# A state-space mixer on one core: log of dt in the decay's bias, output halves summed in SBUF, y's parts first at unit changes, B and C projected a step sooner

## The chip, the cores and the metric

One Trainium2 chip, one core of it. The metric is the device time of one execution in microseconds; less is better. The kernel computes a two-layer network in one launch: attention, a quantized linear layer, a state-space mixer (SSD) and a mixture of low-rank experts, each with a residual and a layer norm behind it. 1024 tokens (2 sequences of 512), 512 channels.

## What is computed

Only the mixer is touched by the change. The reference, cut to it:

```python
dt = softplus(dt + dt_bias); dA = dt * A                    # A = -exp(A_log); 128 heads of 64, 8 groups
cum = cumsum(dA)                                            # within a chunk
Ldec[i, j] = exp(cum[i] - cum[j]) where j <= i, else 0
scores = (C @ B^T) * Ldec * dt[j];  y_intra = scores @ x
dlast = exp(cum[last] - cum); states = (dt * dlast * B)^T x;  cdec = exp(cum[last])
y_inter = (C * exp(cum)) @ state before the chunk;  y = y_intra + y_inter + D * x
g = y * silu(gate)                                          # gate, x, B, C: projections; x, B, C convolved with 4 taps
g = g * rsqrt(mean over the group's 1024 channels of g*g + eps) * norm_w
out = g @ out_w.T
```

## The kernel before, in words

The mixer runs 8 groups. A group has two units (halves) of 8 heads, 512 channels, and a unit walks over 8 chunks of 128 tokens, `c` = 0 to 7, four of each sequence. So a group is 16 steps, `k` = 0 to 15, with `half, c = divmod(k, CHUNKS)`, and the mixer is 128 steps. Each engine has its own list of these steps, written out by hand, and semaphores between them. Nothing reorders it: an engine that waits holds up all that stands behind in its list.

**PE** in a step: the gate projection of a later tile (12 matmuls of 512 columns), the carried part `p_inter` (state times C), one projection of x for the next unit (12), in some steps also one of B or C for the next group (12; `Plan` says in which: `extra`), then `project_out` of the step before (12, from `yT` and `w_out` to `p_out`), the chunk's state (`p_state`), the transposes of x (`p_flip`), and the step's own intra-chunk product (16 small matmuls to `p_intra`). At c = 0 and c = 7 the order is different: at k = 0 and 8 the gate projection comes first, then at once `project_out`; at k = 7 and 15 `project_out` comes behind the intra product.

**DVE** in a step: `mean_square` of two steps back; in half 1 `out_halves` (adds the unit's first half from SBUF to `p_out`, L1926); `arguments` of the next step (L1898: the smaller of two cumulated decays for 8 heads, one instruction of 1024 elements); in half 0 copies of B and C*B; `y_low_part` of the step before (L1908, the low part of y, which `project_out` waits for); `out_sum` (L1934: `p_out` times the inverse rms of the row, added to `acc`; it frees `p_out`); the carried part (L2000, L2005), the decay of the state (L2007), the convolution taps of what was projected (L806, 3 for each event), a copy for the next weights (`w_x`, L814), the new state (L2045, L2047), and `make_y` (L1945, L1950).

**ACT**: half of the decay exponentials (L1763, 8 of 128 columns, bias minus the own decay), `high_y` (L1738), the other half, then the silu of the gate (L1772), `square_y` (L1744), the last tap (L784), the silu of the convolution (L794), `keep_half` (L1748) in half 0, and `empty_x` (L1731). Exponentials and silu need different tables, so ACT loads a table twice in a step.

**POOL**: x with the weights of the state (`to_state`, L2121), x times dt (`to_scores`, L2126), x times D (`skip_part`, L2099), the inverse rms (L2090), the decay matrix times C*B (`decayed`, L2135, which the intra product waits for), the sums of squares (L2105, L2107), and in steps c = 3 to 6 the low parts of the next weights (L825, L2080).

```python
m = act.activation(decay[:, k % 2, h], decay[:, k % 2, h], ACT.Exp, bias=neg[:, c, head:head + 1])
dve.tensor_tensor(decay[:, k % 2], cumB[:], over(logs[:, 0, c, mine], P), ALU.min).then_inc(arg_done, 1)
pool.tensor_tensor(xdt[:], xtok[:], over(dtg[:, c, mine], HEAD_P), ALU.mult).then_inc(xdt_done, 1)
```

## Time and profile before

| | |
|---|---|
| time, median of 3 runs | 2162.05 us (2159.94 to 2162.67) |
| the profiled execution: its time, its span | 2163.59 us, 2161.9 us |
| busy: PE, DVE, ACT, POOL | 93%, 75%, 65%, 61% of the span |
| granted TensorE clock, mean | 0.974 |
| chain that ended last, by engine | PE 33%, DVE 23%, POOL 15%, issue 10%, ACT 6% |

"Busy" is the time in which an engine had an instruction in flight; the row of an instruction gives the idle time of its engine ahead of it and the event that ended this. Starts in a timeline are microseconds from the start of the span. Instructions of an engine overlap by some 0.1 us, so the distance from one start to the next says more of the cost than the duration.

### The profile page before, as it was taken

What the parts mean: (1) busy time and instruction counts of PE and PEld (TensorE: products, weight loads), DVE (VectorE), ACT (ScalarE), POOL (GpSimd) and SP (SyncE); (2) the same over time, 40 slices, a digit from 0 to 9 for tenths busy, and PEclk for the clock granted to TensorE, in tenths of its full rate; (3) what the DMA queues carried; (4) which work ended last, traced back from release to release, by engine and by line L of the source; (5) the groups of instructions that cost most, each with busy time, mean ns of one, the idle gap of its engine ahead of it and who ended that gap; (6) DMA issues with size and microseconds to landing.
All of it is one profiled execution on the core that took longest, in us unless ns stands there. A gap on an engine that the chain in (4) does not pass through costs nothing.

```text
span 2161.9 us, 33838 instructions
## 1 busy us (share of the span) xinstructions
PE 2000.6 (93%) x11288; PEld 1537.9 (71%) x11288; DVE 1615.7 (75%) x2927; ACT 1410.7 (65%) x2692; POOL 1324.2 (61%) x1233
## 2 busy tenths in 40 slices
PE   8899996799999998999899999999999999999868
PEld 4666575677777777777777777777777777777655
DVE  5777574577887787787878877787787778777766
ACT  1566524577767777777777768776766777677621
POOL 4455240367757676767576757765876678667651
PEclk9999997899999999999999999999999999999879
DMA  4000010333223323232332222323322323222201
GB/s 166 2 0 0 1 55 20 92 97 110 77 72 104 111 66 99 72 116 74 93 103 84 83 88 94 102 65 96 98 88 79 93 88 102 66 93 83 90 14 40
DMA packets 125707, 166.05 MB, mean 77 GB/s; under 512 B 37777, under 2 KB 88977, under 8 KB 121330
## 3 DMA queue, kind: packets, MB, share of 16 engines
q1 hardware_dynamic: 125554, 164.11, 23.6%
q8 instruction: 84, 1.38, 0.3%
q14 instruction: 69, 0.57, 0.1%
HBM read 159.88 MB, written 4.20 MB: 76 GB/s over the span
## 4 chain that ended last, share of the span: by engine, by line
PE 33%; DVE 23%; POOL 15%; issue 10%; ACT 6%; SPq 0%; DMA 0%; DVEq 0%; POOLq 0%; ACTq 0%
PE p_out L102 10%; DVE conv L806 9%; PE p_gate_intra L102 7%; PE p_mix L102 6%; POOL x_dt L2126 3%; DVE w_out L1880 3%; POOL x_to_state L2121 3%; POOL x_skip L2099 3%; DVE state L2007 3%; PE p_gate_intra L1686 3%; POOL w_gate L2080 2%; PE pM L102 2%; ACT wq_t L1763 1%; DVE x_skip L2005 1%; POOL w_x L825 1%
## 5 line engine op out<-in xcount | busy, mean ns | idle before, releaser
L102 PE MATMUL p_out<-w_out,yT 128*128 128x512 f32 x1536 | 395.2, 407 | 40.6 <-DVE acc L1934 40.5
L102 PEld LDWEIGHTS p_out<-w_out,yT 128*128 128x128 f32 x1536 | 293.7, 193 | 122.6 <-issue 51.6
L2135 POOL TENSOR_TENSOR wq_t<-wq_t,cb 128x1024 f32<-128x1024 f32 x128 | 313.4, 2448 | 98.5 <-ACT wq_t L1763 98.3
L806 DVE SCALAR_TENSOR_TENSOR conv<-p_mix,unit_small,conv 128x511 f32<-128x511 f32 (+2 forms) x384 | 286.4, 746 | 109.7 <-ACT conv L784 100.5
L102 PE MATMUL p_gate_intra<-x_high,w_gate 128*128 128x512 f32 x1024 | 353.9, 407 | 5.8 <-ACT x_and_gate L1772 4.6
L102 PE MATMUL p_mix<-x_high,w_x 128*128 128x512 f32 x1024 | 353.4, 406 | 1.4 <-DVE x_low L1147 1.4
L1763 ACT ACTIVATE wq_t<-wq_t,minus_cum 128x128 f32<-128x128 f32 x1024 | 324.9, 391 | 3.6 <-DVE wq_t L1898 2.2
L794 ACT ACTIVATE x_and_gate<-conv 128x512 f32<-128x512 f32 x128 | 80.8, 631 | 272.4 <-DVE conv L806 272.2
L102 PEld LDWEIGHTS p_gate_intra<-x_high,w_gate 128*128 128x128 f32 x1024 | 194.2, 190 | 46.2 <-issue 5.8
L102 PEld LDWEIGHTS p_mix<-x_high,w_x 128*128 128x128 f32 x1024 | 193.5, 189 | 42.3 <-DVE x_low L1147 1.8
L2121 POOL TENSOR_TENSOR x_to_state<-x_tokens,group_dt_end 128x512 f32<-128x512 f32 x96 | 115.9, 1207 | 171.8 <-ACT x_tokens L1731 171.8
L2126 POOL TENSOR_TENSOR x_dt<-x_tokens,group_dt 128x512 f32<-128x512 f32 x128 | 179.0, 1398 | 45.4 <-PE p_gate_intra L1686 31.5
L1898 DVE TENSOR_TENSOR wq_t<-cum_all,group_logs 128x1024 f32<-128x1024 f32 x128 | 202.2, 1580 | 4.0 <-DMA cum_all<-cum_rows 3.7
L102 PE MATMUL p_mix<-x_low,w_x 128*128 128x512 f32 x512 | 202.2, 395 | 0.0
L102 PE MATMUL p_gate_intra<-x_low,w_gate 128*128 128x512 f32 x512 | 201.0, 393 | 0.0
L825 POOL TENSOR_TENSOR w_x<-w_raw_tiles,w_x 128x512 fp32r<-128x512 f32 x64 | 82.2, 1284 | 127.4 <-DVE w_x L814 127.4
L2099 POOL TENSOR_TENSOR x_skip<-x_and_gate,group_skip 128x512 f32<-128x512 f32 x128 | 153.7, 1201 | 4.0 <-ACT x_and_gate L794 4.0
L1686 PE MATMUL p_gate_intra<-wq_t,x_dt 128*64 128x128 f32 x2048 | 140.9, 280 | 14.3 <-POOL wq_t L2135 14.3
L1763 ACT ACT_TABLE_LOAD x118 | 151.4, 1283 | 2.1
L1772 ACT ACT_TABLE_LOAD x110 | 141.1, 1283 | 1.9
L1686 PEld LDWEIGHTS p_gate_intra<-wq_t,x_dt 128*64 128x64 f32 x2048 | 110.3, 137 | 42.4 <-issue 21.8
L1661 PE MATMUL p_inter_state<-bc_channels,state 128*128 128x128 f32 x768 | 105.3, 281 | 32.6 <-DVE mean_square L1917 19.2
(244 smaller groups left out, 4309.0 us busy)
## 6 DMA issues: line engine op xcount, KB each, us to landing
cum_all<-cum_rows SPq DMA_DIRECT2D x128, 512.0 KB, 3.7
exp_cum<-exp_rows SPq DMA_DIRECT2D x192, 128.0 KB, 3.3
w_staged<-in_w_gate SPq DMA_DIRECT2D x16, 1024.0 KB, 5.4
w_raw_tiles<-in_w_x SPq DMA_DIRECT2D x64, 256.0 KB, 3.0
w_staged<-in_w_out SPq DMA_DIRECT2D x16, 1024.0 KB, 4.9
w_raw_tiles<-in_w_bc SPq DMA_DIRECT2D x16, 256.0 KB, 5.4
x<-in_x SPq DMA_DIRECT2D x1, 2048.0 KB, 18.6
out<-x_and_gate SPq DMA_DIRECT2D x8, 256.0 KB, 2.0
```

The costliest lines, as they stand in the source:

```text
L102: last = pe.matmul(dst, left[a](k), right[b](k), start=k == 0 and n_ == 0, stop=stop and k == tiles - 1 and n_ == 2)
L806: m = dve.scalar_tensor_tensor(self.conv[:, par, back:], self.p_mix[:, bank, 0:SEQ - back], w[:, TAPS - 1 - back:TAPS - back], self.conv[: ...
L825: pool.tensor_tensor(self.wx[:, 1, j], self.raw[:, j % 2], self.wx[:, 0, j].bitcast(F32), ALU.subtract).then_inc(self.x_w_split, 1)
L1661: m = pe.matmul(p_inter[:, j * P:(j + 1) * P], state[:, 2 * j:2 * j + 2].rearrange("p h e -> p (h e)"), BC[:, 1, cols], start=True, stop=True)
L1686: m = pe.matmul(p_intra[a * HEAD_P:(a + 1) * HEAD_P, j * P:(j + 1) * P], xdt[:, h], decay[:, k % 2, h], start=True, stop=True)
L1763: m = act.activation(decay[:, k % 2, h], decay[:, k % 2, h], ACT.Exp, bias=neg[:, c, head:head + 1])
L1772: act.activation(tile_of(SG, phase, j), p_gate.rearrange("p (q t) -> p q t", t=P), ACT.Silu).then_inc(sg_done, 1)
L1898: dve.tensor_tensor(decay[:, k % 2], cumB[:], over(logs[:, 0, c, mine], P), ALU.min).then_inc(arg_done, 1)
L2099: pool.tensor_tensor(xskip[:], chunk_of(X, c // CPS, c % CPS), over(dg[:, half], P), ALU.mult).then_inc(xskip_done, 1)
L2121: pool.tensor_tensor(xs[:], xtok[:], over(dtend[:, c, mine], HEAD_P), ALU.mult).then_inc(xs_done, 1)
L2126: pool.tensor_tensor(xdt[:], xtok[:], over(dtg[:, c, mine], HEAD_P), ALU.mult).then_inc(xdt_done, 1)
L2135: pool.tensor_tensor(decay[:, k % 2], decay[:, k % 2], cb[:, c].unsqueeze(1).to_broadcast([P, UNIT_HEADS, P]), ALU.mult).then_inc(decay_do ...
```

## The change

1. **Log of dt as bias.** The layer ahead of the mixer makes log(dt + 1e-30) on ACT and puts it into the table where dt stood. In the mixer dt then reaches the scores through the exponent: exp(min(cum_i, cum_j) - cum_j + log dt_j). `arguments` becomes 8 instructions of 128 columns (min, then subtract, both with the head's own column as a per-partition operand), and the exponentials take log dt as their bias. `to_scores` goes away, with its tile `xdt` and its semaphore; the intra product reads `xtok`, which now has two buffers. The tables and D have two buffers too and are read in place; the copies of them at a group's start go away.
2. **Output halves.** `out_halves` writes its sum to SBUF (`half_out`) and so frees `p_out` itself. `out_sum` goes from DVE for all but the last group: ACT scales the sum by the inverse rms (`scale_out`, 56 times), and POOL adds it to `acc` (`add_out`, 56 times), one to three steps later.
3. **y's parts first.** At c = 0 `y_low_part` stands at the head of DVE's step, and `high_y` goes to the end of the step before on ACT, between the halves of the exponentials. In the other steps `square_y` stands ahead of the gate's silu. `arguments` of a group's step 0 come early in step 15, and at c = 0 those of step 1 right behind `out_halves`.
4. **B and C sooner.** Three projections of B and C in half 1 go from c = 4, 5, 6 to c = 3, 4, 5.
5. On POOL at c = 0 and 4, `to_state` goes ahead of `skip_part`.

```diff
-            extra = {(0, 0): ("bc", 1, 1), (1, 4): ("bc", 0, 0), (1, 5): ("bc", 0, 1), (1, 6): ("bc", 1, 0)}
+            extra = {(0, 0): ("bc", 1, 1), (1, 3): ("bc", 0, 0), (1, 4): ("bc", 0, 1), (1, 5): ("bc", 1, 0)}
...
+                act.wait_ge(const2, 3)
+                act.wait_ge(stats_done, 4 * CHUNKS + 1)
+                act.activation(log_dt[:], dt[:], ACT.Ln, bias=head_small[:, 3:4]).then_inc(soft, 1)
...
-                            m = pe.matmul(p_intra[a * HEAD_P:(a + 1) * HEAD_P, j * P:(j + 1) * P], xdt[:, h],
+                            m = pe.matmul(p_intra[a * HEAD_P:(a + 1) * HEAD_P, j * P:(j + 1) * P], xtok[:, k % 2, h],
...
+                def scale_out(g, c):
+
+                    act.wait_ge(out_free, step(g, CHUNKS + c) + 1)
+                    act.wait_ge(rms_done, g * CHUNKS + c + 1)
+                    act.activation(half_out[:, c], half_out[:, c], ACT.Copy, scale=rms[:, c:c + 1]).then_inc(out_scaled, 1)
...
+                        square_y(*before)
                         if s + AHEAD < TILES:
                             silu_gate(s)
-                        square_y(*before)
...
-                                decay_exps(s + 1, (k + 1) % STEPS)
+                                decay_exps(s + 1, (k + 1) % STEPS, 0, UNIT_HEADS // 2)
+                                high_y(g, k)
+                                decay_exps(s + 1, (k + 1) % STEPS, UNIT_HEADS // 2)
...
-                    mine = slice(half * UNIT_HEADS, (half + 1) * UNIT_HEADS)
-                    dve.tensor_tensor(decay[:, k % 2], cumB[:], over(logs[:, 0, c, mine], P), ALU.min).then_inc(arg_done, 1)
+                    for h in range(UNIT_HEADS):
+                        head = half * UNIT_HEADS + h
+                        own = tab[:, s // STEPS % 2, 0, c, head:head + 1]
+                        m = dve.tensor_scalar(decay[:, k % 2, h], cumB[:, h], own, own, ALU.min, ALU.subtract)
+                    m.then_inc(arg_done, 1)
...
-                    dve.tensor_tensor(p_out[:], p_out[:], half_out[:, c], ALU.add).then_inc(halves_done, 1)
+                    dve.tensor_tensor(half_out[:, c], p_out[:], half_out[:, c], ALU.add).then_inc(out_free, 1)
...
+                        if c == 0 and before:
+                            y_low_part(*before)
                         if older:
                             mean_square(*older)
                         if older and older[1] >= CHUNKS:
                             out_halves(*older)
...
-                        if older and older[1] >= CHUNKS:
-                            out_sum(*older)
...
+                def add_out(g, c):
+
+                    at_ = g * CHUNKS + c
+                    pool.wait_ge(out_scaled, at_ + 1)
+                    pool.tensor_tensor(acc[:, c], acc[:, c], half_out[:, c], ALU.add).then_inc(acc_done, 1)
...
-                        def to_scores():
-                            wait(pool, intra_done, s)
-                            pool.tensor_tensor(xdt[:], xtok[:], over(dtg[:, c, mine], HEAD_P),
-                                               ALU.mult).then_inc(xdt_done, 1)
```

DVE at a middle step of half 0 (from `mean_square` on; `wq_t` is the decay matrix, `yT` the low part of y, `sum_squares` the reading of the squares). Before:

```order
L1915 COPY sum_squares<-p_inter_state 128x1
L1898 TENSOR_TENSOR wq_t<-cum_all,group_logs 128x1024
L1981 COPY b_tokens<-p_mix 128x128
L1982 TENSOR_TENSOR cb<-p_mix,causal 128x128
L1908 TENSOR_TENSOR yT<-p_gate_intra,yT 128x512
```

and now:

```order
L1945 COPY sum_squares<-p_inter_state 128x1
L1928 TENSOR_SCALAR wq_t<-cum_all,tables_in 128x128 x8
L2010 COPY b_tokens<-p_mix 128x128
L2011 TENSOR_TENSOR cb<-p_mix,causal 128x128
L1938 TENSOR_TENSOR yT<-p_gate_intra,yT 128x512
```

The place of the arguments is the same, ahead of the low part of y; one instruction has become eight.

POOL at the same kind of step (c = 5), from the low parts of the weights on. Before:

```order
L825 TENSOR_TENSOR w_x<-w_raw_tiles,w_x 128x512
L2080 TENSOR_TENSOR w_gate<-w_staged,w_gate 128x512
L2121 TENSOR_TENSOR x_to_state<-x_tokens,group_dt_end 128x512
L2126 TENSOR_TENSOR x_dt<-x_tokens,group_dt 128x512
L2099 TENSOR_TENSOR x_skip<-x_and_gate,group_skip 128x512
L2135 TENSOR_TENSOR wq_t<-wq_t,cb 128x1024
```

and now:

```order
L826 TENSOR_TENSOR w_x<-w_raw_tiles,w_x 128x512
L2099 TENSOR_TENSOR w_gate<-w_staged,w_gate 128x512
L2147 TENSOR_TENSOR x_to_state<-x_tokens,group_exps 128x512
L2118 TENSOR_TENSOR x_skip<-x_and_gate,skip_in 128x512
L2156 TENSOR_TENSOR wq_t<-wq_t,cb 128x1024
```

One instruction of 512 columns has gone from POOL's stream; three to five of its instructions still stand ahead of the decay product.

DVE where a group ends and the next begins (taps of step 15, then step 0; `attn` is the SBUF tile of the halves). Now:

```order
L807 SCALAR_TENSOR_TENSOR conv<-p_mix,unit_small,conv 128x509
L1938 TENSOR_TENSOR yT<-p_gate_intra,yT 128x512
L1947 TENSOR_SCALAR mean_square<-p_inter_state,sum_squares 128x1
L1950 TENSOR_SCALAR mean_square<-mean_square 128x1
L1956 TENSOR_TENSOR attn<-p_out,attn 128x512
L2010 COPY b_tokens<-p_mix 128x128
L2011 TENSOR_TENSOR cb<-p_mix,causal 128x128
L1928 TENSOR_SCALAR wq_t<-cum_all,tables_in 128x128 x8
```

Before, the last instruction that freed `p_out` there (L1934) stood behind seven others, two of them copies of tables and one of them the arguments; now `p_out` is free with the fourth.

## Rows read from the trace of the kernel before

**Rows 1.** The page: busy time, share of the span, instructions of each engine.

```profile
PE 2000.6 (93%) x11288; PEld 1537.9 (71%) x11288; DVE 1615.7 (75%) x2927; ACT 1410.7 (65%) x2692; POOL 1324.2 (61%) x1233
```

**Rows 2.** What PE waited for, longest total first: us, times, longest.

```profile
PE p_out L102 <- DVE acc L1934: 40.5, 25, 3.6
PE p_inter_state L1661 <- DVE mean_square L1917: 19.2, 10, 4.4
PE p_gate_intra L1686 <- POOL wq_t L2135: 14.3, 16, 3.7
PE p_inter_state L1661 <- DVE sum_squares L1915: 13.3, 8, 1.7
```

**Rows 3.** Timeline of DVE at the change from group 3 to 4.

```profile
1241.19 0.70 DVE L1950 TENSOR_TENSOR p_gate_intra<-p_gate_intra,x_and_gate 128x512 f32<-128x512 f32 x1
...
1247.47 0.74 DVE L1934 SCALAR_TENSOR_TENSOR acc<-p_out,inv_rms,acc 128x512 f32<-128x512 f32 x1
```

**Rows 4.** Timeline of PE there: start, us, idle before and its releaser.

```profile
1248.36 4.51 PE L102 MATMUL p_out<-w_out,yT 128*128 128x512 f32 x12 [2.94 <-DVE acc L1934]
```

**Rows 5.** The stretch behind it: us, busy of each engine, PEclk, DMA share, GB/s.

```profile
1250.00:1255.00 5.00, 5.00 (x19) 3.89 (x19) 0.33 (x1) 1.57 (x3) 1.68 (x2) 0.71 0.22 67
```

**Rows 6.** Timeline of DVE at the mixer's start.

```profile
396.06 1.31 DVE L1887 TENSOR_SCALAR minus_cum<-tables_in 128x128 f32<-128x128 f32 x1
397.29 1.31 DVE L1888 COPY group_logs<-tables_in 128x128 f32<-128x128 f32 x1
...
401.08 0.22 DVE L1964 COPY group_dt<-tables_in 128x128 f32<-128x128 f32 x1
```

**Rows 7.** Timeline of POOL at the mixer's start.

```profile
394.78 4.97 POOL L2080 TENSOR_TENSOR w_gate<-w_staged,w_gate 128x512 fp32r<-128x512 f32 x4 [0.16 <-ACT w_gate L1715]
```

**Rows 8.** Timelines of DVE elsewhere: TENSOR_SCALAR with two per-partition operands, and its successor.

```profile
326.62 0.54 DVE L1134 TENSOR_SCALAR acc<-acc,ln_mv,ln_rstd 128x512 f32<-128x512 f32 x1
327.08 0.68 DVE L1147 TENSOR_TENSOR srcT<-pT,srcT 128x512 fp32r<-128x512 f32 x1
...
2104.89 0.30 DVE L1375 TENSOR_SCALAR bc_channels<-bc_channels 128x28 f32<-128x28 f32 x1
2105.10 0.29 DVE L1376 TENSOR_SCALAR bc_channels<-bc_channels 128x28 f32<-128x28 f32 x1
```

**Rows 9.** Timeline of DVE, group 3, from the end of step 5 to that of 6.

```profile
1112.14 0.42 DVE L814 CAST w_x<-w_raw_tiles 128x512 fp32r<-128x512 f32 x1
...
1113.27 0.70 DVE L1945 TENSOR_TENSOR p_gate_intra<-p_gate_intra,x_skip 128x512 f32<-128x512 f32 x1
...
1114.75 1.51 DVE L1898 TENSOR_TENSOR wq_t<-cum_all,group_logs 128x1024 f32<-128x1024 f32 x1
...
1117.54 0.69 DVE L1908 TENSOR_TENSOR yT<-p_gate_intra,yT 128x512 fp32r<-128x512 f32 x1 [0.89 <-ACT yT L1738]
...
1122.00 2.30 DVE L806 SCALAR_TENSOR_TENSOR conv<-p_mix,unit_small,conv 128x511 f32<-128x511 f32 x3
...
1125.53 0.70 DVE L1945 TENSOR_TENSOR p_gate_intra<-p_gate_intra,x_skip 128x512 f32<-128x512 f32 x1 [0.29 <-PE p_gate_intra L1686]
```

**Rows 10.** Timeline of ACT in that step.

```profile
1117.42 1.27 ACT L1763 ACTIVATE wq_t<-wq_t,minus_cum 128x128 f32<-128x128 f32 x4
1118.70 1.28 ACT L1772 ACT_TABLE_LOAD   x1
...
1120.97 0.78 ACT L784 ACTIVATE conv<-p_mix,unit_small 128x512 f32<-128x512 f32 x1
```

**Rows 11.** Timeline of POOL in that step.

```profile
1113.88 1.30 POOL L2080 TENSOR_TENSOR w_gate<-w_staged,w_gate 128x512 fp32r<-128x512 f32 x1
1115.14 2.02 POOL L2121 TENSOR_TENSOR x_to_state<-x_tokens,group_dt_end 128x512 f32<-128x512 f32 x1
...
1118.13 1.04 POOL L2099 TENSOR_TENSOR x_skip<-x_and_gate,group_skip 128x512 f32<-128x512 f32 x1
1119.12 2.41 POOL L2135 TENSOR_TENSOR wq_t<-wq_t,cb 128x1024 f32<-128x1024 f32 x1
```

More of the change, by code:

```diff
@@ L645, in events @@
         for e in self.steps[k]:
-            if not (last and k >= CHUNKS + CPS):
+            if not (last and (k >= CHUNKS + CPS or (k >= CHUNKS and e[0] == "bc"))):
                 out.append((e, fill, conv))
@@ L1489, in n_feeds, with n_decays @@
             return g * (2 * PER_HALF) + sum(feeds(i % CHUNKS) for i in range(k))
+        def n_decays(g, k):
+            return g * (2 * SEQS * (CPS - 2)) + sum(feeds(i % CHUNKS) and carries(i % CHUNKS) for i in range(k))
         def step(g, k):
@@ L1856, in group @@
                             keep_half(*before)
+                        if half and c > 1 and not last:
+                            scale_out(g, c - 2)
+                        if k in (1, 2) and not first:
+                            scale_out(g - 1, CHUNKS - 3 + k)
                         if (k + 1) % CPS:
@@ L1975, in group @@
                             out_halves(*older)
-                        if c > 1 and k + 1 < STEPS:
-                            arguments(s + 1, k + 1)
+                        if c > 1 and not (last and k == STEPS - 1):
+                            arguments(s + 1, (k + 1) % STEPS)
                         if half == 0:
@@ L2006, in group @@
                             if feeds(c):
+                                if k == 1:
+                                    dve.wait_ge(exps_done, g + 1)
                                 dve.tensor_tensor(state[:], state[:], over(exps[:, 1, c, mine], HEAD_P),
                                                   ALU.mult).then_inc(state_steps, 1)
+                        if last and half and c > 1:
+                            out_sum(g, c - 2)
                         if k == STEPS - 1 and not last:
[L2010 to L2013 removed]
+                            end_logs(g + 1)
                         if half and c in (1, 2) and not last:
@@ L2041, in group @@
                             if carries(c):
-                                per = SEQS * (CPS - 2)
-                                before_ = sum(feeds(i % CHUNKS) and carries(i % CHUNKS) for i in range(k))
-                                dve.wait_ge(state_steps, g * (2 * per) + before_ + 1)
+                                dve.wait_ge(state_steps, n_decays(g, k) + 1)
                                 dve.tensor_tensor(flat, p_state[:], flat, ALU.add).then_inc(state_done, 1)
@@ L2150, in group @@
                             sum_squares(s - 1)
+                        if half and c > 2 and not last:
+                            add_out(g, c - 3)
+                        if k in (1, 2, 3) and not first:
+                            add_out(g - 1, CHUNKS - 4 + k)
                         if last and k == 2 * CHUNKS - 1:
```

159 lines of the change are left out of this document (78 added, 81 removed).

## The prediction

> **What bounds the kernel now.** I read the page first. PE is busy for 93% of the span [rows 1], no other engine for more than 75%; 160 us is all that a change can take from PE's idle time, since none of PE's matmuls goes. Then the list of PE's waits, to see which of them the change touches. Four stand out [rows 2]: 40.5 us for `acc` (L1934), which frees `p_out`; 19.2 and 13.3 us for the reading of the mean square, with DVE late; 14.3 us for the decay product on POOL, at steps 7 and 15. Then timelines of one group. The mixer repeats itself to 0.1 us from group to group: in most steps PE never waits, and 9 us of waits in a group of some 210 us sit at steps 0, 1, 7, 9, 10 and 15. So the question is twofold: which of these waits go, and whether the new work on DVE makes steps late that are now set by PE.
>
> **Gains, on the path.**
>
> *`p_out` at a group's start.* At the change of group PE stands idle for 2.94 us until `acc` is written, at 1248.36 [rows 4]. DVE ends y at 1241.9 [rows 3]; by the new order there follow the taps (2.2 us, as the distance in [rows 9] from 1122.00 to the end less the overlap), the low part of y, the mean square and `out_halves` (0.6, 0.3 and 0.6), so `p_out` is free near 1245.6, when PE is just through with the gate at 1245.4. The wait goes but for 0.2 or less; with seven changes of group, 7 x 2.94 = **-20.6 us**. Behind four of the seven the granted clock fell: 0.71 over 5 us [rows 5], a mix of both levels (2.4 and 1.2 GHz), after PE had been idle 2.94 us. If PE does not stand, that does not come: 5 x 0.29 = 1.45 us, 4 times, **-5.8 us**.
>
> *`p_out` elsewhere.* 40.5 - 20.6 leaves 20 us of the first wait of [rows 2], 0.64 each at steps 1 and 10 of seven groups and the rest in the last group. I take the two, 14 x 0.64 = **-9 us**; in the last group PE will wait for the low part of y instead.
>
> *Head.* DVE's scan of dt*A waits for ACT's softplus and a small exponential with a table of its own; the new order has that exponential ahead of the table change, so one load of 1.28 us (as in [rows 10]) goes from the path: **-1.3 us**. The new Ln runs on ACT beside the scan: nothing.
>
> **The cost that I weigh most: one instruction becomes eight.** Alone, the eight would be harmless. With two per-partition operands a TENSOR_SCALAR takes 0.46 us to its successor at 512 columns and 0.21 at 28 [rows 8]; on the line between, 128 columns are 0.26, eight are 2.1 us. The one instruction now took 1.43 in this step [rows 9], of which some wait.
>
> But DVE and POOL get in each other's way. At the mixer's start, while POOL runs four instructions in a row [rows 7], DVE's TENSOR_SCALAR and COPY of 128 columns take 1.31 us each, one ending just after each of POOL's; with POOL idle the same copy takes 0.22 [rows 6]. So each small DVE instruction waited out a whole instruction of POOL. The Trainium skill states this as a rule (SBUF — State Buffer, "Who interferes with whom": VectorE's two-port modes, and its instructions with two SBUF inputs, share a port pair with GpSimd, and whoever comes second is blocked for the whole instruction of the other). By that rule the trace agrees, and the present argument instruction pays as well: POOL's `x_to_state` takes 2.02 us where its neighbour takes 1.0 [rows 11]. The difference is that one instruction waits once and eight can wait eight times.
>
> How often, in the steps c = 5 and 6, where POOL is fullest? Take T = 1112.14, the end of the taps, from which both chains start. POOL's `w_gate` ends at T + 3.0 [rows 11]. With x times dt gone and nothing to wait for, `x_to_state` ends at T + 4.05 and `x_skip` at T + 5.05 (1.0 each, as 1118.13 to 1119.12). The arguments are ready to start at T + 2.6: the first gets through at T + 3.05, the second at 4.1, the third at 5.1, and then POOL is idle until the exponentials are done. The eighth starts at 5.1 + 5 x 0.26 = T + 6.4. ACT's exponentials end at 1118.69, T + 6.55 [rows 10]. **So all eight get through 0.15 us before POOL starts the decay product of 2.4 us** [rows 11]. This margin decides the case. I forecast that it holds, because POOL needs some 0.05 us more to wake.
>
> Even then the low part of y starts at T + 7.0 (0.4 us for the two small copies) where it stood at T + 5.4 (1117.54 [rows 9]). It hardly holds up `project_out`, which PE reaches some 7.2 us into a step. But `square_y` now stands ahead of the silu's table load on ACT and waits for it: square to T + 8.15, load 1.28, silu 0.5, last tap 0.8, so the taps can start at T + 10.75 and end at T + 13.0, where they start at 1122.00 = T + 9.86 and end at T + 12.1 [rows 9]. PE's step is 12.26 (1113.27 to 1125.53, the second time with DVE waiting for PE [rows 9]). **The chain of DVE and ACT gets 0.7 us longer than PE's step, and was shorter.** It had 1.3 us in hand; two such steps use that up and it shows at step 7, whose decay product PE already waits 0.7 us for (14.3 / 16 to 20 of [rows 2]): I put 1.4 us there in each group. In half 1 the loop with B and C taps is 15.2 against 14.8 of PE, and the step after it, now without B and C, 13 against 12: again some 1.4 us, and it takes up what moving B and C would have given at step 15. (8 + 7) x 1.4 = **+21 us**.
>
> At step 9 the low part of y, behind the arguments, comes 0.3 us after PE wants it: 7 x 0.3 = **+2**. In the last group's steps 13 and 14 POOL has a backlog when the arguments run, so the fourth waits out the decay product; low part of y 1.2 us later than `acc` is now, twice, less 1.0 for x times dt at step 15: **+1.4**.
>
> **At nothing:** `scale_out` (0.5 us on ACT, in place of `keep_half` in half 1 at most steps; it has no more cover at c = 2 to 6 than the 0.15 above, and is counted in the loop of half 1), `add_out` on POOL (1.0, replaces the 1.0 of x times dt; hidden in POOL's idle time, 39% [rows 1]), out of DVE 0.65 each for `out_sum` (it would be the price if its cover were gone; here it is behind the low part of y). The table copies of a group's start: 0.3 us of DVE, behind the taps; POOL's start at step 0 no longer waits for them, and nobody waits for POOL there. DMAs are the same in number and size, to the other buffer.
>
> The eight are nowhere in this trace together with their surroundings. Bounds: below, they cost no port at all (2.1 to 2.6 us flat, as without POOL), and the +21, +2 and +1.4 go; above, the eighth misses everywhere. I take the count in between, from the nearest rows, and keep both ends.
>
> **Sum:** -20.6 - 5.8 - 9 - 1.3 + 21 + 2 + 1.4 = -12.3 us. The profiled execution's 2163.6 becomes 2151.3; it stood 1.5 above the median of the runs shown, 2162.05, so the forecast is **2150 us**.
>
> The Trainium skill has a second rule against the change: an instruction with an SBUF source pays a fixed latency (VectorE: DVE Perf Modes, the section on the TRN2 errata: 58 cycles at 0.96 GHz plus the columns over the mode's factor). By its figures eight would be an estimated 8 x 0.13 = 1.0 us, not 2.1, and the margin above 0.8 us. The rows show 0.21 at 28 columns [rows 8], and they decide.
>
> **The rivals.**
>
> *The decay product comes first (slower, 0.30).* If the eighth argument is 0.15 us later than I count, POOL takes the port at T + 6.6 and the argument ends at T + 9.1. Low part, square, silu and taps all move by 2.5 us; it decides from the point where third to eighth take over 1.45 us. For it: the margin is smaller than the error of the 0.26. Against: exponentials and arguments hang on the same T, so lateness does not add up. Sites are steps 5, 6, 13, 14. At two of them: 16 x 2.5 = +40, **2190 us**; at all four 2230.
>
> *The eight hardly meet POOL (faster still, 0.16).* If they pass two at a time between instructions of POOL, or take one port only, they are done before the exponentials with a microsecond in hand, and the lateness of square and silu is 0: -12.3 - 24.4 = -36.7, **2125 us**. For it: PE's waits that go are certain. Against: the 1.31 of [rows 6].
>
> *It evens out (0.12).* The product comes first at one site of the four in some groups, 5 to 6 times 2.5 us: within 0.2% of 2162, that is 4.3 us, about what a measurement of this kernel can tell from no change.
>
> **How the numbers follow.** Forecast 0.42 (2140 to 2158, all faster), the second rival 0.16, the third 0.12, the first 0.30. Faster 0.58, same 0.12, slower 0.30. The range goes from 2120 (the second rival with the wait at step 15 gone too) to 2200 (the first at two sites, somewhat beyond); outside are all four sites and a little below, under 0.2. The forecast's own range is 2140 to 2158.
>
> **What would show it.** Right: PE's wait at the start of groups under 0.5 us and no fall of the clock behind it; x8 arguments that take 3.5 to 4.5 us in steps 5 and 6, the first three each ending with an instruction of POOL, the eighth just ahead of the decay product; PE's waits for that product over 2 us at steps 7 and 15. Wrong by the first rival: an argument of over 2 us at steps 5, 6, 13 or 14, PE waiting there for `yT`. Wrong by the second: arguments under 2.6 us everywhere and PE's waits at steps 7 and 15 as before. It would be wrong as a whole if PE's busy time changed, since no matmul did.

## The result and the profile after

The changed kernel takes **2169.1 us** (median of 6 runs, 2167.21 to 2171.56) against 2162.21 before: a ratio of 1.0033, 95% interval 1.0016 to 1.0049. It is slower by 7 us, where 12 less were forecast. The profiled execution took 2171.56 us, its span is 2169.7.

The page of the changed kernel, busy time of each engine (compare [rows 1]):

```profile
PE 2001.8 (92%) x11288; PEld 1539.6 (71%) x11288; DVE 1759.9 (81%) x3728; ACT 1451.0 (67%) x2756; POOL 1174.5 (54%) x1161
```

PE's work is the same. DVE has 144 us more, POOL 150 us less. What PE waited for (us in all, times, longest; compare [rows 2]):

```profile
PE p_gate_intra L1694 <- POOL wq_t L2156: 34.5, 16, 2.4
PE p_out L102 <- DVE yT L1938: 22.3, 25, 4.4
PE p_inter_state L1669 <- DVE mean_square L1947: 19.3, 10, 4.4
PE p_inter_state L1669 <- DVE sum_squares L1945: 13.8, 8, 2.0
```

The 40.5 us for `acc` are gone. In their place stand 22.3 us for the low part of y (`yT`), and the decay product is waited for 34.5 us instead of 14.3. Where the first went shows at the change of group, on PE (start, us, idle before):

```profile
1249.95 1.09 PE L1694 MATMUL p_gate_intra<-wq_t,x_tokens 128*64 128x128 f32 x16 [2.21 <-POOL wq_t L2156]
...
1257.09 2.92 PE L102 MATMUL p_out<-w_out,yT 128*128 128x512 f32 x12
```

`p_out` follows the gate without a gap, where PE stood 2.94 us [rows 4]. But PE now stands 2.21 us one product earlier, at step 15. At the first change of group (0 to 1) such a wait, of 2.38 us, ended at 616.60; this is the stretch behind it (PEclk is the column behind POOL's):

```profile
617.00:622.00 5.00, 5.00 (x26) 3.97 (x23) 3.98 (x6) 3.15 (x8) 1.99 (x3) 0.66 0.01 3
```

0.66 is a mix of 1.2 and 2.4 GHz, as in [rows 5]. Ahead of the last group's final steps the trace has six such falls of the clock, three of them at step 7 and three at step 15; before there were four, all at a group's start, the last of them twice as long as the others.

Now the eight. All arguments together, before and after (count, busy us, mean ns):

```profile
L1898 DVE TENSOR_TENSOR wq_t<-cum_all,group_logs 128x1024 f32<-128x1024 f32 x128 | 202.2, 1580 | 4.0 <-DMA cum_all<-cum_rows 3.7
```

```profile
L1928 DVE TENSOR_SCALAR wq_t<-cum_all,tables_in 128x128 f32<-128x128 f32 x1024 | 406.6, 467 | 4.1 <-DMA cum_all<-cum_rows 4.1
```

A set takes 3.18 us on average instead of 1.58. The spread of a single one of the eight (ns, shortest, median, longest):

```profile
L1928 DVE TENSOR_SCALAR wq_t<-cum_all,tables_in x1024: 328/337/2531, 400.3 to 2077.7; 128x128 f32<-128x128 f32 x171
```

Those of about 2.5 us, the length of the decay product, stand at steps 0 and 8 of nearly every group, and two more (2.38) at steps 13 and 14 of the last. Step 6 of group 3, DVE (compare [rows 9]):

```profile
1119.88 0.42 DVE L815 CAST w_x<-w_raw_tiles 128x512 fp32r<-128x512 f32 x1
...
1122.28 4.03 DVE L1928 TENSOR_SCALAR wq_t<-cum_all,tables_in 128x128 f32<-128x128 f32 x8
1126.23 0.28 DVE L2010 COPY b_tokens<-p_mix 128x128 f32<-128x128 f32 x1
1126.43 0.28 DVE L2011 TENSOR_TENSOR cb<-p_mix,causal 128x128 f32<-128x128 f32 x1
1126.63 0.68 DVE L1938 TENSOR_TENSOR yT<-p_gate_intra,yT 128x512 fp32r<-128x512 f32 x1
...
1130.55 2.32 DVE L807 SCALAR_TENSOR_TENSOR conv<-p_mix,unit_small,conv 128x511 f32<-128x511 f32 x3 [0.74 <-ACT conv L785]
1132.79 0.42 DVE L815 CAST w_x<-w_raw_tiles 128x512 fp32r<-128x512 f32 x1
```

POOL and ACT in that step (compare [rows 10, 11]):

```profile
1122.89 1.06 POOL L2147 TENSOR_TENSOR x_to_state<-x_tokens,group_exps 128x512 f32<-128x512 f32 x1
1123.89 1.05 POOL L2118 TENSOR_TENSOR x_skip<-x_and_gate,skip_in 128x512 f32<-128x512 f32 x1
1126.86 2.41 POOL L2156 TENSOR_TENSOR wq_t<-wq_t,cb 128x1024 f32<-128x1024 f32 x1 [1.91 <-DVE cb L2011]
```

```profile
1127.34 0.60 ACT L1752 ACTIVATE y_squares<-p_gate_intra 128x512 f32<-128x512 f32 x1 [0.91 <-DVE yT L1938]
1127.96 1.28 ACT L1791 ACT_TABLE_LOAD   x1
...
1129.75 0.77 ACT L785 ACTIVATE conv<-p_mix,unit_small 128x512 f32<-128x512 f32 x1
```

With T = 1119.88 the eight take 4.03 us, the low part starts at T + 6.75, the cycle closes at T + 12.91. The forecast had 3.5 to 4.5, 7.0 and 13.0. One line is new: the decay product waits for `cb`, which stands behind the eight on DVE. And the square waits 0.91 us, ahead of table load, silu and last tap. PE feels the late low part of y in the same group, at steps 4, 6 and 14, where it did not wait for it before:

```profile
1101.08 3.05 PE L102 MATMUL p_out<-w_out,yT 128*128 128x512 f32 x12 [0.42 <-DVE yT L1938]
...
1127.36 3.02 PE L102 MATMUL p_out<-w_out,yT 128*128 128x512 f32 x12 [0.43 <-DVE yT L1938]
...
1235.37 3.03 PE L102 MATMUL p_out<-w_out,yT 128*128 128x512 f32 x12 [0.73 <-DVE yT L1938]
```

The lengths of the steps, from one end of `p_gate_intra`'s 16 products (L1686, L1694) to the next, us, group 3 (the clock at full speed in all that are shown):

| step | 0 | 4 | 5 | 6 | 7 | 10 | 11 | 14 | 15 |
|---|---|---|---|---|---|---|---|---|---|
| before | 20.58 | 12.44 | 12.26 | 12.26 | 8.92 | 12.98 | 10.70 | 14.80 | 8.70 |
| after | 17.27 | 13.27 | 12.52 | 12.89 | 10.22 | 11.91 | 13.34 | 13.25 | 10.32 |

Steps 0 and 10 give 4.4 us, 4 to 7 take 3.0, 15 takes 1.6, and B and C's move adds 2.6 at 11 and gives only 1.6 at 14. Of the 7.8 us between the two profiles 6.5 lie in the mixer. Its first intra-chunk product starts 3.2 us later, and 3.0 of that are there after the first 50 us, in code that did not change; the tail behind the mixer is 1.8 us shorter.

### The profile page after: what moved, and what is told of

Its sections match the earlier page's. It is cut to its first block, busy times and chain, and to the rows that moved or that the text cites. A ratio compares the mean times of both kernels' runs of the same rounds, so it can differ in the third digit from the quotient of the medians.

```text
span 2169.7 us, 34649 instructions
## 1 busy us (share of the span) xinstructions
PE 2001.8 (92%) x11288; PEld 1539.6 (71%) x11288; DVE 1759.9 (81%) x3728; ACT 1451.0 (67%) x2756; POOL 1174.5 (54%) x1161
## 4 chain that ended last, share of the span: by engine, by line
DVE 30%; PE 26%; ACT 20%; issue 8%; POOL 2%; SPq 0%; DMA 0%; ACTq 0%; DVEq 0%; POOLq 0%
DVE conv L807 11%; DVE wq_t L1928 7%; PE p_out L102 7%; PE p_gate_intra L102 6%; PE p_mix L102 5%; ACT L1791 4%; ACT wq_t L1781 3%; DVE w_out L1906 3%; ACT conv L785 2%; ACT L1781 2%; ACT x_and_gate L1791 2%; PE p_gate_intra L1694 2%; PE pM L102 2%; POOL wq_t L2156 2%; DVE p_gate_intra L1975 2%
## 5 line engine op out<-in xcount | busy, mean ns | idle before, releaser
L2156 POOL TENSOR_TENSOR wq_t<-wq_t,cb 128x1024 f32<-128x1024 f32 x128 | 308.3, 2408 | 298.9 <-ACT wq_t L1781 263.1
L102 PE MATMUL p_out<-w_out,yT 128*128 128x512 f32 x1536 | 394.7, 408 | 22.6 <-DVE yT L1938 22.3
L1928 DVE TENSOR_SCALAR wq_t<-cum_all,tables_in 128x128 f32<-128x128 f32 x1024 | 406.6, 467 | 4.1 <-DMA cum_all<-cum_rows 4.1
L1781 ACT ACTIVATE wq_t<-wq_t,tables_in 128x128 f32<-128x128 f32 x1024 | 326.1, 390 | 4.9 <-DVE wq_t L1928 3.4
L2147 POOL TENSOR_TENSOR x_to_state<-x_tokens,group_exps 128x512 f32<-128x512 f32 x96 | 100.8, 1050 | 171.1 <-ACT x_tokens L1739 171.1
L1694 PE MATMUL p_gate_intra<-wq_t,x_tokens 128*64 128x128 f32 x2048 | 141.8, 281 | 34.5 <-POOL wq_t L2156 34.5
L2118 POOL TENSOR_TENSOR x_skip<-x_and_gate,skip_in 128x512 f32<-128x512 f32 x128 | 140.2, 1096 | 31.8 <-DVE p_gate_intra L1975 31.7
L1694 PEld LDWEIGHTS p_gate_intra<-wq_t,x_tokens 128*64 128x64 f32 x2048 | 110.6, 138 | 63.2 <-POOL wq_t L2156 41.3
L1669 PEld LDWEIGHTS p_inter_state<-bc_channels,state 128*128 128x128 f32 x768 | 100.1, 195 | 51.3 <-issue 46.3
```

The source lines that it names most:

```text
L102: last = pe.matmul(dst, left[a](k), right[b](k), start=k == 0 and n_ == 0, stop=stop and k == tiles - 1 and n_ == 2)
L1669: m = pe.matmul(p_inter[:, j * P:(j + 1) * P], state[:, 2 * j:2 * j + 2].rearrange("p h e -> p (h e)"), BC[:, 1, cols], start=True, stop=True)
L1694: m = pe.matmul(p_intra[a * HEAD_P:(a + 1) * HEAD_P, j * P:(j + 1) * P], xtok[:, k % 2, h], decay[:, k % 2, h], start=True, stop=True)
L1928: m = dve.tensor_scalar(decay[:, k % 2, h], cumB[:, h], own, own, ALU.min, ALU.subtract)
L2118: pool.tensor_tensor(xskip[:], chunk_of(X, c // CPS, c % CPS), over(skip[:, g % 2, half], P), ALU.mult).then_inc(xskip_done, 1)
L2147: pool.tensor_tensor(xs[:], xtok[:, k % 2], over(exps[:, 0, c, mine], HEAD_P), ALU.mult).then_inc(xs_done, 1)
```

## The experiments

The theory, from the traces: **the eight make DVE's low part of y late, and the square, which now stands ahead of the silu on ACT, passes that on to the taps (E)**. The rival: the orders cost by themselves and the eight are hidden (O). Each experiment was timed side by side with the kernel before; ratios are to that.

**One argument instruction again (a1_one_argument).** The own sum, subtracted by the eight, is folded into the bias instead (log dt minus the sum); that rounds log dt away where the sum is large, so this kernel and the fourth corner below compute other, wrong decays, by the same amount of work. They measure what the eight cost and cannot be used as kernels.

```diff
-    for h in range(UNIT_HEADS):
-        m = dve.tensor_scalar(decay[:, k % 2, h], cumB[:, h], own, own, ALU.min, ALU.subtract)
+    dve.tensor_tensor(decay[:, k % 2], cumB[:], own, ALU.min)
```

> The changed kernel with the arguments as one TENSOR_TENSOR min again; the own cum goes into the exponentials' bias (log dt minus cum, subtracted once a group in place), everything else as changed. Theory E (the eight instructions make DVE's chain late; the arguments took 406.6 us of DVE instead of 202.2): DVE busy falls by some 200 us, PE's 34.5 us of waits for the decay product fall to 15 or less, the steps k = 4 to 7 go back to before's lengths (13.28, 12.50, 12.89, 10.22 to 12.44, 12.26, 12.26, 8.92: 3.0 us a group) and those of half 1 give 1.8 us a group; time 2169 - 38 = 2131, at least under 2145. Rival O (the lateness comes from the new orders, square ahead of silu and B/C a step sooner, the eight are hidden): 2169 to 2160, PE's waits for the decay product stay over 25 us.

2116.6 us, ratio 0.9783 (0.9767 to 0.9799). Steps 4 to 7 went back to 12.54, 12.19, 12.19 and 9.18 us, as E had it, and ahead of the last group's final steps the clock never fell. DVE's busy time fell by 134.6 us, not 200: `state` times its exponential takes longer instead (2.22 us each against 1.34 with the eight). PE still waited 24.8 us for the decay product, not 15, and the time is below E's 2131; rival O, which had 2160 or more, is out.

**The eight alone, in the kernel before (a2_eight_alone).** The same edit the other way round, on `before`.

> The kernel before with nothing but the arguments changed: eight TENSOR_SCALARs (min, subtract) in place of one TENSOR_TENSOR, exponentials without the bias. Theory E: POOL is fuller here (x times dt is still there), so the arguments take 3.2 us or more a set and the time goes up by 25 to 50 us, to 2187 to 2212. Rival O: within 5 us of 2162. Rival P (the port race that the prediction made its first rival: the decay product is taken up before the eighth argument): arguments of over 2 us each for a single one in steps 5, 6, 13 or 14, and 2200 or more.

**2337 us**, ratio 1.080 (1.0785 to 1.0816), far beyond E's range; only P's "2200 or more" holds it. PE's first wait, and DVE and POOL at a group's start:

```profile
PE p_out L102 <- DVE acc L1937: 128.8, 41, 7.9
```

```profile
1098.01 5.03 DVE L1900 TENSOR_SCALAR wq_t<-cum_all,group_logs 128x128 f32<-128x128 f32 x8
1102.96 0.75 DVE L1937 SCALAR_TENSOR_TENSOR acc<-p_out,inv_rms,acc 128x512 f32<-128x512 f32 x1
```

```profile
1098.09 2.34 POOL L2138 TENSOR_TENSOR wq_t<-wq_t,cb 128x1024 f32<-128x1024 f32 x1
1100.38 1.04 POOL L2102 TENSOR_TENSOR x_skip<-x_and_gate,group_skip 128x512 f32<-128x512 f32 x1
```

The decay product is taken up 0.08 us behind the first argument, the eight wait out it and `x_skip`, and `acc`, which frees `p_out`, stands behind them. This is the mechanism of the first rival of the prediction (P). It is seen at steps 13 and 14, which that rival named (single arguments of 2.43 us), but not at 5 and 6, and what costs most is this place, a group's start, which it did not name. So whether the eight are cheap is decided by what stands behind them.

**Arguments of half 0 behind `b_tokens` and `cb` (a3_behind_cb).**

```diff
-if c > 1 and not (last and k == STEPS - 1):
+if half and c > 1 and not (last and k == STEPS - 1):
     arguments(s + 1, (k + 1) % STEPS)
...
-if c < 2:
+if c < 2 or half == 0:
     arguments(s + 1, k + 1)
```

> The changed kernel with the arguments of half 0 behind b_tokens and cb of the same step (as they are at c = 0 and 1) instead of ahead of them. In the changed kernel POOL's decay product of half 0 waits 1.91 us for cb, which stands behind the eight. Theory C (that wait is what makes the decay product late in steps 2 to 7): PE's 34.5 us of waits for the decay product lose the part of half 0 (about 16 us), time 2169 - 10 to -16 = 2153 to 2159. Rival E' (DVE's sum of work decides, not this order): b_tokens and cb move ahead but the low part of y stays where it was, time within 4 us of 2169; it could be worse, if the decay product now starts while arguments are still under way and blocks them for 2.4 us.

2159.9 us (2152.19 to 2166.87 in 12 runs), ratio 0.9992 (0.9979 to 1.0005): 9 us off the changed kernel by the medians, just outside theory C's range (2153 to 2159). Steps 5 and 6 became 12.2 and 12.4, step 7 stayed at 10.2 and PE's wait for the decay product at 34.6 us. So the wait for `cb` was real, but it was not what made that product late. This run also settles the race of the prediction: with `cb` out of the way the decay product of steps 5 and 6 waits for the exponentials alone, and it starts 0.2 us behind the end of the eighth argument (1100.72 against 1100.49, and 1113.20 against 1112.99).

**The square behind the silu again (a4_square_behind).**

```diff
-square_y(*before)
 if s + AHEAD < TILES:
     silu_gate(s)
+square_y(*before)
```

> The changed kernel with the square of y behind the gate's silu again (as before), all else as changed. Theory S (the square waits 0.9 us for the low part of y ahead of the silu's table load, and silu, last tap and taps of the steps with eight arguments come later by it): steps 5 to 7 shorter by 0.5 to 1 us each, 2169 - 8 to -16 = 2153 to 2161. Rival (that time is given back since the square and so the mean square come 1.3 + 0.5 us later, and PE already waits 33 us for the mean square and the sum of squares): 2165 to 2175.

(The same two calls are put back at c = 0.) **2130.5 us**, ratio 0.9844 (0.9830 to 0.9859): 39 us from the place of one call, more than twice what S expected. The groups of the square on ACT, changed kernel and this one (the last number: idle before it), and PE's waits here:

```profile
L1752 ACT ACTIVATE y_squares<-p_gate_intra 128x512 f32<-128x512 f32 x128 | 75.8, 592 | 51.5 <-DVE yT L1938 48.9
```

```profile
L1752 ACT ACTIVATE y_squares<-p_gate_intra 128x512 f32<-128x512 f32 x128 | 75.8, 592 | 15.4 <-DVE yT L1938 15.4
```

```profile
PE p_gate_intra L1694 <- POOL wq_t L2156: 22.9, 16, 2.9
...
PE p_out L102 <- DVE yT L1938: 12.1, 9, 4.4
```

33.5 us of ACT's waiting went. PE's waits at steps 7 and 15 fell to 1.1 and 1.6 us, and with them went the falls of the clock: one instead of the six. A group takes 205.5 us instead of 211.1 (209.5 where the clock held).

**The fourth corner: one argument and the square behind (b2_one_square).**

> The fourth corner of a square: one argument instruction (with the own cum subtracted from log dt in the bias, as in a1_one_argument) and the square of y behind the silu. Known: eight and square ahead 2169, eight and square behind 2130, one and square ahead 2117. Theory I (both act through the same thing, DVE's low part of y coming late ahead of the silu, so whoever takes away one gets most of it): 2105 to 2115, that is the square's place costs under 10 us once the arguments are short. Rival A (the two add up): 2117 - 39 = 2078.

2118.0 us, ratio 0.9787 (0.9772 to 0.9802). Theory I came out, if 3 us above its range, and with it theory E: beside one instruction the square's place is worth nothing (2116.6 and 2118.0), beside eight 39 us. The eight themselves cost 12.5 us once the square is behind.

**B and C's projections back at their steps (a5_bc_back),** and **the arguments of half 0 behind `cb` (c1_square_cb)**, both with the square behind.

```diff
-(1, 3): ("bc", 0, 0), (1, 4): ("bc", 0, 1), (1, 5): ("bc", 1, 0)
+(1, 4): ("bc", 0, 0), (1, 5): ("bc", 0, 1), (1, 6): ("bc", 1, 0)
```

> The changed kernel with the square of y behind the silu (a4_square_behind, 2130) and B and C's projections back at steps c = 4, 5, 6 of half 1. Theory B (the move gives back the wait at step 15, as the prediction had it): PE's wait for the decay product at step 15, 1.6 us, grows by 0.5 to 1.5 and the time is 2134 to 2142. Rival N (the move is worth nothing once the low part of y is in time): 2127 to 2133; rival L (it costs, since it makes step 11 to 13 full): below 2126.

> The changed kernel with the square of y behind the silu and the arguments of half 0 behind b_tokens and cb. a3_behind_cb alone gave some 9 us (2169 to 2160, with a spread of 15 us), the square's place 39. Theory C: the low part of y and the decay product of half 0 stay a little late in the kernel with the square behind (steps 4, 5 and 7 are 0.4, 0.3 and 0.2 us over the shortest), so at most 8 x 0.5 = 4 us more: 2125 to 2130. Rival: the later arguments now delay the exponentials of the next step and step 7 grows: 2131 to 2140.

2130.4 us (0.9840, 0.9822 to 0.9858): rival N, that part of the change is worth nothing; step 15 has 9.56 us in both. 2129.0 us (0.9836, 0.9822 to 0.9849) with the order of a3: as theory C had it, little is left for `cb`.

**dt multiplies x on POOL again,** one argument instruction, bias minus the sum, square behind; first with `x_to_state` made from `x_dt` (c2_x_dt_square), then ahead of it from `x_tokens`, as before (d4_x_dt_state_first).

> The changed kernel with its first part undone and the rest kept: dt multiplies x on POOL again (x_dt, 1.0 us a step), the arguments are one TENSOR_TENSOR, the decays' bias is minus cum, x_to_state is made from x_dt, no Ln of dt; and the square of y behind the silu. Theory E (the eight are what costs DVE its slack, POOL at 55% has room for the 128 us): DVE busy under 1640, PE's waits at the start of a group 0 as in the changed kernel, time 2108 to 2122. Rival P (POOL's chain to the decay product at steps 7 and 15 gets 1 us longer and PE waits for it): p_gate_intra waits over 30 us, 2130 to 2145.

> c2_x_dt_square (2166) with x_to_state made from x_tokens ahead of x_dt, as before the change (dt times the end's exponential once a group on DVE). In c2 PE waited 21 us for x_to_state and the clock fell behind that wait at k = 4. Theory Q (that order was the fault of c2, POOL's 128 us are harmless): 2115 to 2130. Rival P (POOL's chain x_to_state, x_dt, x_skip, decay product is too long by itself with DVE's one argument instruction blocking it for its length, log dt in the decays is worth the rest): 2145 to 2170.

2165.8 us (1.0013, 1.0002 to 1.0025), beyond both of its ranges, and 2147.3 us (0.9934, 0.9921 to 0.9947), rival P. The order of my first version was the fault for 18 us; what is left against 2118.0 (the kernel with the wrong decays) says that dt in the decays, and 128 instructions of 1.0 us less on POOL, are worth 29 us. In the second, PE waits 2.5 us at step 15, and three groups begin at the lower clock.

**DVE's low part of y ahead of the arguments in every step (d1_low_ahead),** square ahead as changed.

```diff
-if c > 1 and not (last and k == STEPS - 1):
-    arguments(s + 1, (k + 1) % STEPS)
...
 if c and before:
     y_low_part(*before)
+if not (last and k == STEPS - 1):
+    arguments(s + 1, (k + 1) % STEPS)
```

> The changed kernel, square of y still ahead of the silu, but DVE's low part of y ahead of the eight arguments in every step (b_tokens and cb ahead of both in half 0). Theory W (what the square's place costs is the time ACT stands in front of it, waiting 0.91 us for the low part that lies behind the eight; with the low part in time the order square, silu does no harm): the wait of y_squares for yT is under 0.2 us, PE's waits for yT in groups 1 to 7 go, the time is 2125 to 2137. Rival T (it is the square's own 0.6 us ahead of the table load, silu and taps): at most a third of the 39 us comes back, 2150 to 2165. Rival X (the arguments, 0.7 us later, now meet the decay product: a single one of over 2 us in steps 5, 6, 13, 14): 2170 or more.

**2449 us**, ratio 1.133 (1.131 to 1.134). Rival X, and far beyond the "2170 or more" that I had put on it. DVE and POOL, group 3, step 6:

```profile
1248.28 0.69 DVE L1938 TENSOR_TENSOR yT<-p_gate_intra,yT 128x512 fp32r<-128x512 f32 x1 [2.53 <-ACT yT L1746]
1248.89 4.92 DVE L1928 TENSOR_SCALAR wq_t<-cum_all,tables_in 128x128 f32<-128x128 f32 x8
```

```profile
1249.50 2.50 POOL L2154 TENSOR_TENSOR wq_t<-wq_t,cb 128x1024 f32<-128x1024 f32 x1 [1.62 <-ACT wq_t L1781]
```

The arguments had filled the 2.5 us for which DVE must wait for ACT's high part anyway. Moved out of them, they meet the decay product in 124 of 128 sets: 696 us for all, 5.44 each, and single ones of up to 2.6 us, the product's length. So this run says nothing on theories W and T: its new cost covers whatever the square's place gave back.

**The two other parts undone,** each on the kernel with the square behind: the low part of y behind the arguments at the change of units (d2_y_low_behind),

```diff
-if c == 0 and before:
-    y_low_part(*before)
...
-if c and before:
+if before:
     y_low_part(*before)
```

> a4_square_behind (2130) with one more part undone: at the change of units (c = 0) DVE's low part of y stands behind the mean square, the output halves and the arguments again. Theory G (this order is what took away PE's 2.94 us at the group's start, the prediction's -20.6): PE waits 2 to 5 us at k = 0 and the clock falls behind it in some groups, 2150 to 2175. Rival (it is the sum of halves into SBUF that freed p_out, the order of the low part is worth little): below 2138.

and the output halves in PSUM, scaled and added by DVE, behind the low part of y (g1_halves_back).

```diff
-dve.tensor_tensor(half_out[:, c], p_out[:], half_out[:, c], ALU.add)
+dve.tensor_tensor(p_out[:], p_out[:], half_out[:, c], ALU.add)
...
+dve.scalar_tensor_tensor(acc[:, c], p_out[:], rms[:, c:c + 1], acc[:, c], ALU.mult, ALU.add)
```

> a4_square_behind (2130) with the second part of the change undone: DVE adds the halves in PSUM, waits for the inverse root, and multiplies and adds into acc itself, behind the low part of y; no scale_out on ACT, no add_out on POOL. Theory H (the sum in SBUF is what frees p_out early, together with y's parts first): PE waits for acc at k = 0, 1, 9 to 14 again, 1 to 5 us each, the clock falls behind the longest, 2160 to 2230. Rival (with y's parts first the halves' place does not matter): within 6 us of 2130.

2199.0 us (1.0175, 1.0161 to 1.0189) and 2226.0 us (1.0276, 1.0253 to 1.0299). PE's first wait in each:

```profile
PE p_out L102 <- DVE yT L1938: 59.1, 25, 4.4
```

```profile
PE p_out L102 <- DVE acc L1957: 81.2, 32, 5.6
```

The first is above its theory's range (2150 to 2175), the second within it. Beside the eight these two parts are worth 68 and 95 us. Step 0 takes 23.9 and 24.5 us instead of 17.2, with waits of 3.7 and 4.9 us: the rest, 3.0 and 2.4, is the clock behind them. What remains lies at step 8 in the first (2.65 us of waiting, no fall of the clock) and at step 14 in the second (3.6 us and a fall in every group).

**Two long instructions in place of the eight (h1_two_tensors),** on the last-group version below.

```diff
+dve.tensor_tensor(decay[:, k % 2], cumB[:], own, ALU.min)
+dve.tensor_tensor(decay[:, k % 2], decay[:, k % 2], own, ALU.subtract)
```

> d3_last_group (2123) with the arguments as two TENSOR_TENSORs over 1024 columns, min and then subtract, the same numbers as the eight. Theory C (the count of instructions sets the price: two can be blocked twice, eight up to eight times; unblocked both take 2.1 to 2.3 us): arguments 2.4 to 2.9 us a set instead of 3.2, PE's waits at k = 13, 14 and in the last group smaller, 2113 to 2121. Rival W (long instructions hold the port for 1.1 to 1.6 us each and block POOL and wait for whole POOL instructions with twice the data: arguments 3.2 us or more a set): 2124 to 2140.

2139.5 us (0.9875, 0.9852 to 0.9898): rival W. Here are DVE's two, and POOL's `x_skip` here and with the eight:

```profile
L1929 DVE TENSOR_TENSOR wq_t<-wq_t,tables_in 128x1024 f32<-128x1024 f32 x128 | 229.1, 1790 | 4.4
L1927 DVE TENSOR_TENSOR wq_t<-cum_all,tables_in 128x1024 f32<-128x1024 f32 x128 | 192.3, 1502 | 4.1 <-DMA cum_all<-cum_rows 4.1
...
L2120 POOL TENSOR_TENSOR x_skip<-x_and_gate,skip_in 128x512 f32<-128x512 f32 x128 | 194.0, 1515 | 35.4 <-DVE p_gate_intra L1975 35.3
```

```profile
L2120 POOL TENSOR_TENSOR x_skip<-x_and_gate,skip_in 128x512 f32<-128x512 f32 x128 | 140.1, 1095 | 34.0 <-DVE p_gate_intra L1975 33.9
```

3.29 us a set, and now POOL's instructions take longer too. So the number of instructions was not the price. Undisturbed, the shortest two take 1.21 and 1.22 us, together 2.43 against 2.13 for the eight; that the rest goes by the data moved over a shared port is my reading and was not tested by itself.

**The last group (d3_last_group, n1_last_exps),** towards the best version: on the kernel with both orders mended, steps 13 to 15 take the mean square, the halves and the low part first and the norms of the step before after them; then also ACT's eight exponentials in one piece there.

> c1_square_cb (2129) with another order in the last group's steps 13 to 15, on DVE alone: mean square, output halves, low part of y, then the norms of the step before (that stood at the end of that step, ahead of the mean square), then the arguments. In c1 PE waits there 4.0 and 4.4 us for the mean square and 4.4 and 4.5 us for the low part. Theory: 12 to 18 us of these go, 2111 to 2117. Rival (the norms only move: POOL's reciprocal roots and the x_to_state behind them come late, or the tail after the last group grows by what is gained): 2122 to 2129.

> d3_last_group (2123) with ACT's eight exponentials of the last group's steps 13 to 15 all ahead of the high part of y (elsewhere four, high part, four). In d3 PE waits 4.9 us for the decay product at step 15, whose second four exponentials stand behind the high part of y while ACT is idle for 3.3 us. Theory: that wait falls under 1.5 us, 2118 to 2121. Rival (the decay product then waits for something else, POOL or cb, or the tail takes it up): 2121 to 2125.

**2123.1 us** (0.9821, 0.9808 to 0.9833) and 2122.8 us (0.9802, 0.9778 to 0.9826). The first gave 6 us of the 12 to 18, which is its rival's range, the second nothing: PE's 4.9 us for the decay product at step 15 stayed. They are 38 and 42 us under the kernel before, each in its own comparison, and some 46 under the change. What that last wait hangs on stays open.

## Why the prediction was wrong

The terms of the sum beside what the steps of the two profiled executions show (us, all groups; negative is faster). The clock's share is an estimate, from the groups in which it fell against those in which it held.

| term | forecast | measured |
|---|---|---|
| `p_out` at a group's start (step 0) | -20.6 | -23.2 |
| falls of the clock at steps 0 and 8 | -5.8 | +0.6 |
| `p_out` elsewhere (steps 1 and 10) | -9 | -13.5 |
| step 9 | +2 | +2.0 |
| lateness at steps 7 and 15 | +21 | +22.6 |
| lateness at steps 4, 5 and 6 | 0 | +11.8 |
| steps 11 to 14, groups 0 to 6 | 0 | +7.8 |
| last group, steps 11 to 15 | +1.4 | +0.3 |
| steps 2, 3 and 8 | 0 | -1.9 |
| up to the mixer (3.0 of it in unchanged code) | -1.3 | +3.2 |
| behind the mixer | 0 | -1.8 |
| sum | -12.3 | +7.8 |

The first steps of its sum held. **`p_out` at a group's start:** PE's idle time there is 0.00, step 0 is 3.3 us shorter; undoing either part that does it costs 68 or 95 us beside the eight. **`p_out` elsewhere** gave more than forecast: steps 1 and 10 are 0.7 and 1.1 us shorter. **Step 9** is 0.23 us longer.

**The head**, -1.3, came to nothing. The table load went, and PE's wait for the scan fell from 6.4 to 5.3 us, but PE then waited 4.9 us instead of 3.3 for ACT's copies of the table. The new Ln waits 2.14 us for dt on DVE, and what is queued behind it on ACT waits with it; "the new Ln runs on ACT beside the scan: nothing" overlooked that. No run tested this by itself.

**The clock**, -5.8, was not gained. "If PE does not stand, that does not come" fits a4, which has one fall instead of six, but in the changed kernel PE stood 2.0 us at step 7 and 2.2 to 2.4 at step 15, and the clock fell behind some of those waits. I had forecast the waits themselves ("over 2 us at steps 7 and 15") and had not asked what they would do to the clock.

**The lateness, +21, is the step that failed.** Its cause was right: 4.03 us, T + 6.75 and T + 12.91 where 4.0, 7.0 and 13.0 stood. Steps 7 and 15 even have the size forecast. What failed is "two such steps use that up and it shows at step 7". It showed already at steps 4, 5 and 6, with 0.8, 0.3 and 0.6 us in a group: at 4 and 6 PE waited 0.4 us for the low part of y, and at 4 0.58 instead of 0.34 for `x_to_state`. And step 14, which should have given back the 2.64 that step 11 took, gave 1.55, with 0.73 us of waiting for the low part. That is some 19 us more, about the distance between -12.3 and +7.8: the term was sized at 21 and came out at 42. The clock (6) and what lies ahead of the mixer (4.5) came on top; the larger gains at `p_out` (7) and some smaller ones took those back. The experiments split the lateness: the place of the square is worth 39 us, some 7 of falls of the clock included, and the eight alone, with the square behind, 12.5.

The second rival, "the eight hardly meet POOL" (2125), named the time that came out once the square stood behind (2130), for another reason: they meet POOL as forecast, and nothing on the path stands behind them. The first rival, the decay product before the eighth argument, did not occur at steps 5 and 6 of the changed kernel and could not: in half 0 the product waits for `cb`, which DVE reaches only after the eight. So the margin of 0.15 us did not decide this case. Where the order lets it decide, in a3, the eighth got through by 0.2 us, about what I had counted. At steps 13 and 14 the rival occurred only in the last group, as forecast. At steps 0 and 8, which the prediction did not look at, one argument waits out the product in nearly every group (2.5 us) and nothing on the path stands behind it. a2 and d1 show what losing the race costs where something does, 175 and 280 us, many times the 40 that I gave it.

The Trainium skill's rule that VectorE and GpSimd block each other for whole instructions (SBUF — State Buffer, "Who interferes with whom") agrees with these traces: arguments of 2.6 us beside a product of 2.5, and in h1 POOL's `x_skip` longer beside DVE's long ones. Its fixed latency (VectorE: DVE Perf Modes, on the TRN2 errata) gave an estimate of 1.0 us for an undisturbed set; the shortest sets in the trace take 2.13, as the line through [rows 8] had said, and the measurement decides.

Added up from the runs: halves, y first and B and C from 2162 to 2147 (d4), dt in the decays to 2118 (b2, with the wrong decays), eight instead of one to 2130 (a4), the square ahead of the silu to 2169. The last step, one order on ACT, makes the sign.

## What to carry to other kernels

A wait that is placed ahead of a table load delays everything behind it on that engine: price it by the whole chain to the next engine that waits, and in every step that has it, not only in the one where you expect to see it. Small instructions that share a port are cheap only as filler, in time in which their engine would wait anyway; list what stands behind them before and after. Where parts of a change were designed together, measure each beside the others: here the same line is worth nothing or 39 us, and the same eight 12 or 175.

## What the runs showed of the hardware

DVE's arguments and POOL's instructions hold each other up for whole instructions. Where both have work, one argument gets through at each end of an instruction of POOL: arguments of 128 columns come 0.26 us apart where POOL is idle, take 1.08 us each beside instructions of 1.0 (step 6 above), and one takes up to 2.6 beside the decay product. With two instructions of 1024 columns instead of the eight, POOL was slowed as well (`x_skip` from 1.10 to 1.52 us).

The granted clock fell behind, or during, some waits of PE and not others of the same length. Leaving out the last group's final steps, it fell behind three of nine waits of 2.0 us and three of seven of 2.2 to 2.4 in the changed kernel, none of seven of 2.2 in a1, one of seven of 2.25 in b2, none of eight of 2.65 in d2, four of seven of 2.9 to 3.3 in the kernel before, and all of those of 3.6 and 4.9 in d2 and g1. In d4 it even fell behind two of eight of 1.65, a length behind which it did not fall in the kernel before. So in these traces the length of one wait does not tell by itself whether the clock falls. Each fall at a group's start cost 1.5 to 3 us beyond the wait ahead of it.

The mixer's first intra-chunk product started between 417.1 and 427.8 us in the seventeen profiles, and the same spread is there in the layers ahead of it, whose first 350 us run the same code. A single profile is therefore no measure of some us, and the profiles here are compared by steps.
